# A graph network on one core: loads of 56 and 64 node rows, a new order in the attention visits, and 23 visits of 55 target nodes found by groups of eight edges

## What is computed

```python
x = _layernorm(x + x @ W.T + bias)           # W: 1024x1024, scattered from edge_weight at (src, dst)
h = rmsnorm(x) @ W_down                       # 1250x256
xl, xr = h @ Wl, h @ Wr                       # 4 heads of 64
e = einsum(leaky(xl[src] + xr[dst]), att)     # one score for each edge and head
p = exp(e - segment_max(e, dst)[dst])
out = segment_sum(p / segment_sum(p, dst)[dst] * xl[src], dst)
x = _layernorm(x + out @ W_up)
x = _layernorm(x + relu(gcn(x, W) + b))
x = _layernorm(x + two_sage_layers(x))
```

## Time and profile before

| | us |
|---|---|
| median of 3 runs | 1694.56 (1694.53 to 1698.33) |
| the profiled execution's own time | 1698.34 |
| its span | 1696.6 |
| attention stage's first and last `clamp`, start | 427.89 and 777.96 |
| start of the layers stage | 790.02 |

### The profile page before, as it was taken

The page is one execution under the profiler, slowest core; times in us unless marked ns, Lnnn a source line. Parts: engine busy times, 40 slices in busy tenths (PEclk is TensorE's granted clock), DMA queues, the critical chain, the costliest instruction groups (busy, mean ns, idle before and its releaser), DMA issues.

```text
span 1696.6 us, 19105 instructions
## 1 busy us (share of the span) xinstructions
PE 1495.4 (88%) x7184; PEld 1193.5 (70%) x7184; DVE 790.8 (47%) x1352; ACT 442.5 (26%) x723; POOL 245.4 (14%) x298
## 2 busy tenths in 40 slices
PE   3898999506888888887999999999999999999996
PEld 2887888505555555555888888888888888888885
DVE  6996665201666766675444375223113332321233
ACT  7762222103445454542111111002011000210000
POOL 1000000005455544530000001001000010000000
PEclk9997999857999999999999999999999999999998
DMA  1655343013444435432321365224006654410153
GB/s 42 176 166 183 121 104 103 18 49 110 129 156 135 123 106 166 135 96 85 123 107 50 104 229 213 86 96 149 1 0 211 199 174 149 155 37 1 59 183 105
DMA packets 100425, 196.57 MB, mean 116 GB/s; under 512 B 25550, under 2 KB 59638, under 8 KB 100334
## 3 DMA queue, kind: packets, MB, share of 16 engines
q1 hardware_dynamic: 75720, 121.00, 23.2%
q0 software_dynamic: 22992, 74.13, 12.7%
q10 hardware_dynamic: 1622, 0.22, 0.1%
HBM read 141.39 MB, written 53.92 MB: 115 GB/s over the span
## 4 chain that ended last, share of the span: by engine, by line
PE 52%; DVE 0%; ACT 0%; issue 0%; POOL 0%; DVEq 0%
PE layers_y_ps L1764 33%; PE layers_y_ps L1785 16%; PE layers_turn_ps L1748 2%; PE layers_up_ps L1732 2%; PE layers_y_ps L1801 1%; PE layers_turn_ps L1720 0%; PE layers_y_ps L1809 0%; DVE layers_parts_lo L1932 0%; DVE layers_y L1965 0%; POOL out L1705 0%; ACT layers_parts_hi L1876 0%; DVE layers_y L625 0%; DVE layers_y L2027 0%; DVE layers_ln_stats L2031 0%; DVE layers_ln_stats L619 0%
## 5 line engine op out<-in xcount | busy, mean ns | idle before, releaser
L1785 PE MATMUL layers_y_ps<-layers_parts_hi,layers_counts 128*128 128x512 f32 x464 | 143.6, 391 | 0.0
L1170 POOL DMA_INDIRECT attention_got<-xl_d,attention_src x128 | 126.5, 989 | 116.6 <-DVE attention_weighted L1415 69.7
L1785 PE MATMUL layers_y_ps<-layers_parts_lo,layers_counts 128*128 128x512 f32 x464 | 143.3, 390 | 0.0
L1764 PE MATMUL layers_y_ps<-layers_w_hi,layers_parts_hi 128*128 128x512 f32 x400 | 125.9, 396 | 0.0
L1764 PE MATMUL layers_y_ps<-layers_w_lo,layers_parts_hi 128*128 128x512 f32 x400 | 123.6, 390 | 0.0
L1764 PE MATMUL layers_y_ps<-layers_w_hi,layers_parts_lo 128*128 128x512 f32 x400 | 123.5, 390 | 0.0
L1170 POOL DMA_INDIRECT attention_got<-xl_d,heads_first_src x64 | 63.7, 995 | 411.9 <-issue 371.2
L1236 PE MATMUL attention_mix_ps<-attention_weighted,attention_hot 128*106 128x260 f32 x384 | 101.6, 399 | 5.2 <-DVE attention_weighted L1415 5.1
L1236 PEld LDWEIGHTS attention_mix_ps<-attention_weighted,attention_hot 128*106 128x106 f32 x384 | 66.4, 178 | 52.7 <-DVE attention_weighted L1415 24.3
L1201 PE MATMUL attention_row_ps<-attention_bent,edges_att_rows 128*128 128x512 f32 x192 | 102.5, 617 | 0.0
L1363 DVE TENSOR_TENSOR attention_bent<-attention_message_ps,attention_scaled 128x512 f32<-128x512 f32 x96 | 65.8, 686 | 74.0 <-ACT attention_scaled L1300 54.0
(11 more groups left out here) (306 smaller groups left out, 2904.3 us busy)
## 6 DMA issues: line engine op xcount, KB each, us to landing
layers_counts<-counts_d SPq DMA_DIRECT2D x30, 640.0 KB, 4.0
heads_dst_wide<-in_dst_held SPq DMA_DIRECT2D x25, 512.0 KB, 5.9
layers_rest<-x_d SPq DMA_DIRECT2D x23, 512.0 KB, 4.1
x_d<-layers_y POOLq DMA_DIRECT2D x20, 512.0 KB, 2.9
self_d<-layers_y POOLq DMA_DIRECT2D x20, 512.0 KB, 5.5
fetched_x<-x_d SPq DMA_DIRECT2D x17, 512.0 KB, 3.6
fetched_raw<-in_L_gnn_W_self POOLq DMA_DIRECT2D x16, 512.0 KB, 5.7
fetched_raw<-in_L_gnn_W_neigh POOLq DMA_DIRECT2D x16, 512.0 KB, 8.6
```

Of the source, the lines that this page charges most:

```text
L1170: pool.indirect_dma_start(got[s][:, t, :], None, xl_d, bass.IndirectOffsetOnAxis(src[s][:, t:t + 1], 0))\
L1764: last = nc.tensor.matmul(y_ps[n % 2][:, a:a + HALF], rows_in[t][:, k * P:(k + 1) * P], w[k][:, a:a + HALF], start=(k == 0 and p == 0), st ...
L1785: last = nc.tensor.matmul(y_ps[n % 2][:, a:a + HALF], counts[c % 2][:, k, :], part[k][:, a:a + HALF], start=(k == 0 and part is hi), stop= ...
```

## The change

`SUB` becomes 55 and so `SUBS` 23. The subsets' ranges are found by groups of 8 edges (`FINE`), the cells' still by groups of 32. The own rows are loaded as 56 rows and the own scores as 64, whatever `SUB` is; the rows beyond 55 are not used. The `xr` loads take 64 rows, or 32 in the last visit. On DVE `weigh` comes before the quarter's `bend`, two `take_max` before the bend of q = 2, the last `take_max` and `take_best` before the bend of q = 3, and `finish(j - 3)` moves from q = 1 to the end of q = 3. On ACT `take_shifted` comes before `keep_sums`. The last three fetches and the last two splits come one visit earlier.

```diff
-SUB = 53
+SUB = 55
+FINE = 8
+ROW_FINES = GROUP // FINE * ROW_GROUPS
@@ setup
-        sub_hit = m.sb("sub_hit", [P, 2, SUBS, ROW_GROUPS])
+        sub_hit = m.sb("sub_hit", [P, 2, SUBS, ROW_FINES])
-            nc.vector.tensor_copy(starts[:, 0, :], start_i[:, :])
+            nc.vector.tensor_copy(fine_starts[:, 0, :], start_i[:, :])
+            nc.vector.tensor_copy(starts[:, 0, :],
+                                  start_i[:, :].rearrange("p (r f) -> p r f", f=GROUP // FINE)[:, :, 0])
+            nc.vector.tensor_scalar(fine_starts[:, 1, :], fine_starts[:, 0, :], float(FINE), None, ALU.add)
+            nc.vector.tensor_scalar(fine_starts[:, 0, :], fine_starts[:, 0, :], -1.0, FAR_EDGE, ALU.mult, ALU.add)
-            find(sub_nodes, sub_hit, SUBS)
+            nc.vector.tensor_reduce(fine_spans[:, 0, :], dst_held[:, :, :], AX.X, ALU.min)
+            nc.vector.tensor_reduce(fine_spans[:, 1, :], dst_held[:, :, :], AX.X, ALU.max)
+            dve.drain()
+            find(sub_nodes, sub_hit, fine_spans, fine_starts, SUBS, ROW_FINES)
@@ front_stage
-    LAST_ROW = (BLOCKS - 1) * P
+    LAST_ROW, OWN_ROWS = (BLOCKS - 1) * P, 56
         def own_messages(engine, first, end, heads):
-            span = slice(first * SUB, end * SUB)
-            own_xl = xl_d[span, :].rearrange("(j n) (h d) -> n j h d", n=SUB, h=HEADS)
             for h in heads:
-                engine.dma_start(summed[:, first:end, h, 0:HEAD_DIM], own_xl[:, :, h, :]).then_inc(g["own_loaded"], 16)
+                own_xl = bass.AP(xl_d.tensor, first * SUB * HID + h * HEAD_DIM,
+                                 [[HID, OWN_ROWS], [SUB * HID, end - first], [1, HEAD_DIM]])
+                engine.dma_start(summed[0:OWN_ROWS, first:end, h, 0:HEAD_DIM], own_xl).then_inc(g["own_loaded"], 16)
-        def own_scores(engine, first, end, nodes=SUB):
-            span = slice(first * SUB, first * SUB + (end - first) * nodes)
-            scores = loop_d[span, :].rearrange("(j n) (t k) -> t n j k", n=nodes, t=2)
+        def own_scores(engine, first, end, nodes=PART):
             for t in range(2):
-                engine.dma_start(best[t * PART:t * PART + nodes, first:end, :], scores[t])\
+                scores = bass.AP(loop_d.tensor, first * SUB * HEADS + t * KH,
+                                 [[HEADS, nodes], [SUB * HEADS, end - first], [1, KH]])
+                engine.dma_start(best[t * PART:t * PART + nodes, first:end, :], scores)\
@@ last_scores
-                first, end = max(j * SUB, LAST_ROW), (j + 1) * SUB
+                first = max(j * SUB, LAST_ROW)
+                end = min(j * SUB + PART, first + 16 * ((ROWS - first) // 16))
@@ attention_stage
-    FETCH_VISITS, SPLIT_VISITS = (4, 4, 5, 5, 6, 9, 12, 16, 19, 22), (5, 9, 12, 16, 19)
+    FETCH_VISITS, SPLIT_VISITS = (4, 4, 5, 5, 6, 9, 12, 15, 18, 21), (5, 9, 12, 15, 18)
+                held = min(PART, 32 * ((ROWS - j * SUB) // 32))
                 for part in range(2):
-                    sp.dma_start(xr[j % 3][part * PART:part * PART + SUB, :].bitcast(F32),
-                                 xr_d[part][j * SUB:(j + 1) * SUB, :]).then_inc(xr_ready[j % 3], 16)
+                    sp.dma_start(xr[j % 3][part * PART:part * PART + held, :].bitcast(F32),
+                                 xr_d[part][j * SUB:j * SUB + held, :]).then_inc(xr_ready[j % 3], 16)
@@ ACT's loop
                 if q == 3 and 1 <= j <= SUBS:
+                    take_shifted(j - 1)
                     keep_sums(j - 1)
-                    take_shifted(j - 1)
@@ DVE's loop
                 if q == 0 and 2 <= j <= SUBS + 1:
                     clamp(j - 2)
-                if i < LAST:
-                    bend(i)
-                if q == 0 and 2 <= j <= SUBS + 1:
                     weigh(j - 2, 0)
                     weigh(j - 2, 1)
-                if q == 1 and 3 <= j <= SUBS + 2:
-                    finish(j - 3)
                 if q == 2 and 1 <= j <= SUBS:
-                    for u in range(3):
-                        take_max(j - 1, u)
+                    take_max(j - 1, 0)
+                    take_max(j - 1, 1)
                 if q == 3 and 1 <= j <= SUBS:
                     take_max(j - 1, 3)
                     take_best(j - 1)
+                if i < LAST:
+                    bend(i)
+                if q == 2 and 1 <= j <= SUBS:
+                    take_max(j - 1, 2)
+                if q == 3 and 1 <= j <= SUBS:
                     find_edges(j - 1)
                     keep_best(j - 1)
+                if q == 3 and 3 <= j <= SUBS + 2:
+                    finish(j - 3)
@@ graph_layers
-                summed = m.sb("summed", [SUB, SUBS, HEADS, HEAD_DIM + 1])
+                summed = m.sb("summed", [PART, SUBS, HEADS, HEAD_DIM + 1])
```

31 lines of the change are left out of this document (17 added, 14 removed).

## The result

The changed kernel takes **1579.59 us** (median of 4 runs, 1576.18 to 1584.88) against 1696.32 for the kernel before in the same session (4 runs). The ratio is 0.9314, with a 95% interval of 0.9281 to 0.9348. The forecast was 1589 in a range of 1560 to 1620. The profiled execution is the slowest of the four, 1584.88 us, with a span of 1583.1. Against the profiled execution of before (span 1696.6) that is -113.5 us.

The account below looks back on a forecast made before the run. Bounds: SP's unspread loads in the front stage, late first messages, dependence within visits. Terms +1.9 - 42.6 - 15.1 - 8.8 - 40.6 = -105.2 us from the profiled 1698.34 gave 1593.1, or 1589 for the median; range 1560 to 1620.

Parts of the forecast that it names:

- Setup: Setup stage: a second pair of reductions and larger `find` operations delay the field gather; +1.9 us, bounds 0.5 and 3.5.
- ACT at tile 9: End of front stage: own-row loads spread over engines, so ACT takes the last tile at 318.2, not 360.76; -42.6 us.
- the forecast's sign: Listed sign of being right: SP's own-row load commands take near 0.5 us each.
- Tail of the front: From ACT's last tile to the attention stage: 8.5 us instead of 23.6; -15.1 us, bounds -18 and -9.
- First messages: Start of attention stage: gathers set the pace, third message at about +13.5 instead of +22.3; -8.8 us, bounds -5 and -11.5.
- Visits: Attention stage, first to last clamp: 22 intervals sum to 309.5 us against 350.1 before; -40.6 us, bounds 275 and 348.
- L: Time from the `dst_wide` load command on SP to landing; taken as 4.3 us, making a visit 8.9 + L = 13.2.
- No load is late: Rival: L is below 3.5 us, DVE's chain of 12.35 us sets the visits; 1556 us, chance 0.14.
- the loop: Attention visits: `finish`, store, `dst_wide` load, `find_nodes`, scale, bend, `finish` again; 8.9 + L, binding at 13 to 14 us, chance 0.62.
- The order gives nothing: Rival: L stays at 5.9 us, fetches and `load_ahead` cost 29; only the front's gain is left; 1626 us, chance 0.18.
- 56 rows do not spread: Rival: own-message loads hold SP as before, only scores and `xr` gain, about 25 us; 1668 us, chance 0.03.
- Two rounds: Rival: the edge span rounds to two windows of 1024, so the attention stage runs twice; near 1940 us, chance 0.03.

Follow-up runs that it names:

- fourth experiment: The changed kernel with own-message loads of 59 rows instead of 56: 1633.39 us, ratio 0.9633.
- third experiment: The changed kernel with SP storing each subset's result one load later, so that no load waits for `finish`: 1556.17 us, ratio 0.917.
- seventh experiment: The changed kernel, 55 targets kept, with edge ranges found by groups of 32 edges again instead of 8: 1925.03 us in one run.
- tenth experiment: The changed kernel with `keep_sums` alone moved behind the exponentials and first scale of the next visit: 1584.01 us, ratio 0.9325.
- ninth: The third experiment's kernel with `keep_sums` and a split's first half behind the next visit's first scale, its second half one bend later: 1543.01 us, ratio 0.9086.
- second experiment: The changed kernel with the old 53 targets, so 24 visits, stores of 53 rows and fetches at their matching visits: 1621.33 us, ratio 0.9557.

## Why the prediction was right, step by step

**Setup, +1.9:** +1.3 measured. The operations of 552 elements take 0.73 us each and the gather moved to 17.73, as written (17.7); the larger reduction of L237, 1.29 us, was not in the working, but it runs beside the gather.

**ACT at tile 9, -42.6:** 323.14 against 360.76 is -37.6, and everything there stands 4.9 us later, since the norm of that tile does too. So -42.5 of its own. Whether 56 rows go over 14 engines or over 7 could not be told apart, but the fourth experiment shows the rule's other side. The commands were held 0.75 us (own messages) and 1.56 us (scores) each, not near 0.5 as the forecast's sign had it; nothing waits for SP there.

**Tail of the front, -15.1:** from ACT's tile 9 to the next stage it took 23.6 us, now 331.24 - 323.14 = 8.1: -15.5. That it came out so close is partly luck. The heads took the 2.7 us of the forecast; the commands took 3.5 instead of 2.5 (0.70 for a score copy on SP, where 0.5 was taken); landing and barrier took 1.9 instead of 3.3. The stage has -58.7 against -57.7.

**First messages, -8.8:** -10.4. The gathers' landing was taken as 3.9 us from the earlier trace rows and is 2.8. The clock, which the forecast counted at nothing, did rise: 0.77 was granted over these 43.6 us before, 0.95 over the 33.2 now. It can hardly be worth much: in the fourth experiment PE idles 52 us ahead of the stage, the clock is 0.90, DVE's first bend waits for own rows again, and all that together costs 2.1 us up to the first clamp.

**Visits, -40.6:** -49.0, the largest miss in the sum. Its main term, 13.2 us for a plain visit, held (12.97 to 13.3), and so did its reason: L measured 4.2 in the median with 4.3 taken. The rest of the terms were too dear. The first two intervals take 12.7 and 12.1 instead of 14.5 and 13, which is 2.7 us. The last two take 12.1 and 9.9 instead of 12.4 each, 2.8 us. The 18 between sum to 254.2 where 257 were charged (16 of 13.2, two of 12.4, 21 for fetches). The two that were put at 12.4 took 13.0 and, with a fetch, 14.5, so what fetches and splits added to the others was priced too high.

**Sum:** -105.2 forecast and -113.5 found, of which +4.3 is no part of the change. Without it -117.8, 12.6 more than forecast; visits explain 8.4 of it, the tail behind the last clamp 2.2, the first messages 1.6, the front stage 1.0 and setup 0.6, less the 1.1 of the layers stage. The median came out 9 us under the forecast.

**The rivals.** *No load is late* is wrong for this kernel, as ACT's and POOL's waits show, but its price is right: the third experiment makes it true and takes 1556, the very time given. The fit of the Trainium skill, page "DMA: Bandwidth & Descriptors", section "Anatomy of one DMA — SWDGE (gpsimd) path", by which the loop wouldn't bind, is for DMAs issued from GpSimd. It doesn't carry over to these loads from SP's queue: beside a spread store and gathers none of them lands under 3.7 us. The forecast's words that 3.2 us is "below any landing of this trace" hold for the wide loads only; in that trace gathers land in 2.7 us at least, and 512 KB stores (`x_d<-front_y`) in 2.8 in the median. *The order gives nothing* is nearly what the change would have been with its 53-row store, 1621 against 1626 given. What saved it is that 55 has a divisor, which the forecast named for L, but whose weight (29 us of the whole) it didn't price. *56 rows do not spread* is wrong; it is the fourth experiment's 1633. *Two rounds* did not happen, 23 clamps; the seventh experiment shows the price, 1925.

**Not foreseen:** the exchange on ACT was put down as no gain, and a wait that it meets was overlooked. `keep_sums` waits for `finish` of two subsets before, which now ends the visit:

```profile
ACT attention_keep L1330 <- DVE attention_mixed L1452: 48.4, 20, 2.8
POOL attention_got L1184 <- DMA attention_src<-in_src_held: 45.1, 12, 6.2
DVE attention_weighted L1429 <- ACT attention_weighted L1343: 18.9, 20, 1.7
```

These are waits of the changed kernel from 380 to 660 us. The exponentials stand behind `keep_sums` on ACT, and weighing waits 0.9 us a visit for them. In the changed kernel this costs nothing (tenth experiment); once the loads are off the path, it and the split cost 13 us (ninth against third).

## What to carry to other kernels

Count the rows of every DMA: loads of 53 or 59 rows kept the DMA engines 8% busy here and held their queue for tens of microseconds, and a few rows more (56 for 53), or a row split off, repaired that. When work that a store waits for is moved to the end of a loop body, look at what stands behind that store on its queue; issue the store one load later before giving up the new place. And price the place of a movable block by what it covers: `finish` was worth 0.3 to 1.0 us a visit more at the end than in two other places, and that only showed once the queue was out of the way.

## What the runs showed that was not expected

- A small store that doesn't spread delays the loads that follow on its queue. With 53 rows in place of 52 + 1, the 512 KB loads behind it land in 5.3 us instead of 4.2, and the whole kernel is 29 us slower. The same store with no awaited load behind it costs nothing that can be seen.
- Loads that would spread are held by those ahead that don't. In the fourth experiment the two score loads are of 64 rows, and the second row of its fence still shows 15.04 us for them; behind the 56-row loads they took 3.12.
- The gathers land in 2.8 us in the median in the changed kernel, against 3.9 before and 3.8 with the loads changed alone. It isn't the store's engines: with the 53-row store of the second experiment it is 2.8 too. In the kernels with the new order whose loads are not late it is 2.9 to 3.3. So most of it goes with the new order; why was not tried.
